# Cross attention: values held in TensorE on four column tiles, outputs turned back, and a new order of the work around them

## What is computed

```python
x = _layernorm(x + xattn(x, ctx, ctx, Wq, bq, Wk, bk, Wv, bv, Wo, bo))

def xattn(query, key, value, ...):          # 16 heads of 16 channels
    q, k, v = heads(query @ Wq + bq), heads(key @ Wk + bk), heads(value @ Wv + bv)
    scores = einsum('bhqd,bhkd->bhqk', q, k) / sqrt(16)
    x = einsum('bhqk,bhkd->bhqd', softmax(scores), v)
    return join_heads(x) @ Wo + bo
```

## Time and profile before

| | us |
|---|---|
| median of 3 runs | 1328.49 (1326.06 to 1329.64) |
| the profiled execution | 1323.78 |
| its span in the profile | 1321.5 |
| TensorE busy | 1012.9 (77%) |
| VectorE busy | 1027.7 (78%) |
| ScalarE busy | 742.6 (56%) |
| GpSimd busy | 610.1 (46%) |

### The profile page before, as it was taken

The page is one execution under the profiler, slowest core; times in us unless marked ns, Lnnn a source line. Parts: engine busy times, 40 slices in busy tenths (PEclk is TensorE's granted clock), DMA queues, the critical chain, the costliest instruction groups (busy, mean ns, idle before and its releaser), DMA issues.

```text
span 1321.5 us, 25653 instructions
## 1 busy us (share of the span) xinstructions
PE 1012.9 (77%) x7366; PEld 761.2 (58%) x7367; DVE 1027.7 (78%) x2235; ACT 742.6 (56%) x1866; POOL 610.1 (46%) x789
## 2 busy tenths in 40 slices
PE   0335786763698998986888889883799999999980
PEld 0233342432576776763566566652788888888870
DVE  6893899999888988965788888865477777777765
ACT  4784644430678888871455555540366666666650
POOL 3896787775244444431444455543232233322324
PEclk9755987886789989896999999996799999999995
DMA  5953100003133333312022222221011111111105
GB/s 185 383 195 156 48 0 32 0 32 104 55 123 131 117 108 108 108 43 75 1 85 84 83 83 83 79 76 40 25 38 38 36 40 40 34 36 40 40 27 190
DMA packets 51884, 105.69 MB, mean 80 GB/s; under 512 B 9809, under 2 KB 36433, under 8 KB 51329
## 3 DMA queue, kind: packets, MB, share of 16 engines
q1 hardware_dynamic: 47472, 92.39, 20.3%
q0 software_dynamic: 4368, 12.78, 3.2%
HBM read 73.06 MB, written 32.10 MB: 80 GB/s over the span
## 4 chain that ended last, share of the span: by engine, by line
PE 37%; DVE 26%; issue 14%; POOL 6%; ACT 6%; DMA 1%; DVEq 0%; POOLq 0%; SPq 0%; ACTq 0%
PE banks L1985 14%; PE banks L1995 10%; DVE mix_sums L671 4%; ACT att_probs L1484 3%; PE banks L1383 2%; POOL whole L1119 2%; DVE carry L661 2%; DVE whole_stat L227 2%; DVE carry L658 2%; PE banks L1352 2%; DVE kvq L1655 1%; ACT whole_level L1047 1%; PE banks L1360 1%; PE banks L1396 1%; DVE q_sin L1622 1%
## 5 line engine op out<-in xcount | busy, mean ns | idle before, releaser
L2068 DVE SCALAR_TENSOR_TENSOR expert_gate<-banks,expert_steps,expert_chunk 128x128 f32<-128x128 f32 x546 | 166.5, 347 | 96.8 <-ACT expert_chunk L2030 94.5
L1985 PE MATMUL banks<-expert_parts,levels 128*128 128x128 bf16 x3276 | 229.5, 221 | 8.0 <-issue 5.6
L1985 PEld LDWEIGHTS banks<-expert_parts,levels 128*128 x3276 | 203.4, 99 | 48.9 <-issue 21.2
L1995 PE MATMUL banks<-down,up 128*128 x546 | 176.2, 406 | 0.0
L2030 ACT COPY expert_chunk<-banks 128x256 f32<-128x256 f32 x273 | 101.7, 373 | 103.9 <-PE banks L1985 103.8
L2123 POOL DMA_INDIRECT chosen_d<-expert_y,expert_target x39 | 38.9, 998 | 203.9 <-ACT expert_y L2040 203.9
L519 PE MATMUL banks<-x_turned,w_rkv 128*128 128x512 f32 (+1 forms) x192 | 101.6, 690 | 38.9 <-DVE weight L652 38.4
L2034 ACT ACTIVATE silu<-expert_gate,expert_steps 128x128 f32<-128x128 f32 x273 | 110.6, 405 | 15.8 <-DVE expert_gate L2068 15.7
L414 PE MATMUL banks<-consts,level 128*128 128x128 f32 x154 | 35.6, 423 | 87.2 <-POOL level L397 87.2
L2075 DVE SCALAR_TENSOR_TENSOR up<-expert_gate,expert_steps,silu 128x128 f32<-128x128 f32 x273 | 94.6, 347 | 9.3 <-ACT silu L2034 9.3
L1119 POOL TENSOR_TENSOR whole<-whole_level,whole_stat 128x896 bf16<-128x896 f32 x32 | 53.2, 1684 | 102.1 <-DVE whole_level L1188 102.1
(11 more groups left out here) (237 smaller groups left out, 2541.6 us busy)
## 6 DMA issues: line engine op xcount, KB each, us to landing
whole_raw<-in_weight_jobs SPq DMA_DIRECT2D x16, 896.0 KB, 5.2
raw<-in_weight_jobs SPq DMA_DIRECT2D x11, 896.0 KB, 4.9
numbers_d<-turned SPq DMA_DIRECT2D x11, 896.0 KB, 5.1
levels_d<-whole_t SPq DMA_DIRECT2D x16, 448.0 KB, 2.7
levels<-levels_d SPq DMA_DIRECT2D x16, 448.0 KB, 3.6
down<-numbers_d SPq DMA_DIRECT2D x16, 448.0 KB, 4.4
finish_moe<-chosen_d SPq DMA_DIRECT2D x8, 512.0 KB, 7.3
normed_d<-normed_parts SPq DMA_DIRECT2D x16, 192.0 KB, 1.9
```

Source lines behind the costliest of these rows:

```text
L1985: last = pe.matmul(banks[:, at, (m * DC + c) * ROWS:(m * DC + c + 1) * ROWS], levels[:, bass.ds(expert * (2 * JOB) + (m * JOB + (f * DC + ...
L1995: last = pe.matmul(banks[:, Y + j, 0:D], up[j][:, f, :], down[:, bass.ds(expert * JOB + f * D, D)], start=(f == 0), stop=(f == FC - 1))
L2068: last = dve.scalar_tensor_tensor(out=gate[slot(j, f)][:, m, :], in0=halves(at)[:, m, 1, :], scalar=steps[j][:, m, 1, f:f + 1], in1=chunk[ ...
```

## The change

- **Sums.** `v_ones` is widened from 17 to 32 columns (the rest zero) and becomes the stationary operand; the 128 columns of the turned probabilities are moved. The four heads a = 0 to 3 write to the partition bands 32a of PSUM, so to four column tiles of the array. The results of a half (two sets of four heads) lie transposed in the free half of bank V.
- **Outputs turned back.** ScalarE copies them out (`take_outs`, one 128x256 copy a half, to `outs`), and TensorE turns them by two transposes a half (`turn_outs`), into bank HEADS, where `normalise` reads them with a stride of 32.
- **Order.** TensorE: `front` loses its part for the values (`front_v`) and moves ahead of `turn_heads` and behind `turn_probs(0)`; `join(n-1)` moves from the first part of the step to behind `turn_probs(1)` and `turn_outs(0)`, and waits for `take_outs(0, n)`. ScalarE: `take_outs(1, n-1)` leads the step, `back(n-1)` moves behind `take_qk`, `take_outs(0, n)` stands behind `round_part(1)`. GpSimd: `spread_keys` twice, then `add_bias`, then `scale`. VectorE: `normalise(n-1)` moves from the end of a step to behind `peaks(1)` of the next; the join's read (`read_joined`) moves behind the range reductions, and the layer norm (`norm_joined`) behind `peaks(0, n+1)`.

Left out of the diff: the constant `WIDE = 32`, two new semaphores and the last lines of VectorE's program, where `normalise`, `read_joined` and `norm_joined` are called for the last sequence.

```diff
@@ -763,11 +764,12 @@
         spread = [k.buffer(own, f"spread{h}", [QUAD, S]) for h in range(2)]
-        v_ones = [k.buffer(own, f"v_ones{j}", [XH, XK + 1]) for j in range(2)]
+        v_ones = [k.buffer(own, f"v_ones{j}", [XH, WIDE]) for j in range(2)]
         x_bias = [k.buffer(own, f"x_bias{j}", [D]) for j in range(2)]
...
         probs_t = [k.buffer(own, f"probs_t{h}", [HALF, S]) for h in range(2)]
+        outs = [k.buffer(own, f"outs{h}", [2, S]) for h in range(2)]
         total = k.buffer(own, "total", [XH])
@@ -887,8 +891,8 @@
             pe.wait_ge(rows_in[j], 32 * i + 32)
-            if not begin:
-                pe.wait_ge(heads_t_ready, n)
+            if not (isinstance(n, int) and n < 2):
+                pe.wait_ge(whole_read, ROUNDS * (n - 1))
             for c in range(DC):
@@ -904,9 +908,13 @@
             last.then_inc(qk_ready, 1)
-            if not begin:
+        def front_v(j, n):
+            if not (isinstance(n, int) and n == 0):
                 pe.wait_ge(v_read, n)
-                pe.wait_ge(joined_read, n)
+                pe.wait_ge(outs_ready, 2 * n - 1)
+            if not (isinstance(n, int) and n < 2):
+                pe.wait_ge(joined_read, n - 1)
             for c in range(DC):
@@ -930,33 +938,44 @@
-        def sums(j, h, n):
+        def sums(j, h, n, more):
             if h == 0:
-                pe.wait_ge(v_read, n + 1)
-                pe.wait_ge(heads_ready, n + 1)
+                pe.wait_ge(v_read, n + 1 + more)
+            else:
+                pe.wait_ge(joined_read, n + 1)
+            pe.wait_ge(outs_ready, 2 * n + h + 1)
             for m in range(2):
...
                     head = HALF * h + 4 * m + a
-                    last = pe.matmul(banks[:, HEADS, head * (XK + 1):(head + 1) * (XK + 1)], probs_t[h][:, 4 * m + a, :],
-                                     v_ones[j][:, head, :], start=True, stop=True)
+                    last = pe.matmul(banks[WIDE * a:WIDE * (a + 1), V, D + m * S:D + (m + 1) * S], v_ones[j][:, head, :],
+                                     probs_t[h][:, 4 * m + a, :], start=True, stop=True)
+            last.then_inc(outs_summed, 1)
+        def turn_outs(h, n):
+            if h == 0:
+                pe.wait_ge(heads_ready, n + 1)
+            pe.wait_ge(outs_ready, 2 * n + h + 2)
+            for m in range(2):
+                last = pe.transpose(banks[:, HEADS, (2 * h + m) * P:(2 * h + m + 1) * P], outs[h][:, m, :], k.ident)
             if h:
...
             pe.wait_ge(heads_ready, n + 2)
-            pe.wait_ge(x_t_ready, n + 1 + more)
+            pe.wait_ge(x_t_ready, n + 2 + more)
             pe.wait_ge(whole_read, ROUNDS * n + ROUNDS)
...
-        def join(j, n, more):
+        def join(j, n, taken):
             pe.wait_ge(heads_t_ready, n + 2)
-            pe.wait_ge(v_read, n + 1 + more)
+            pe.wait_ge(outs_ready, taken)
             for c in range(DC):
@@ -980,33 +999,41 @@
             if prev:
-                turn_heads(1 - j, n - 1, 1)
+                turn_outs(1, n - 1)
             turn_probs(0, n)
+            if more:
+                front(1 - j, n + 1, i + 1)
             if prev:
-                join(1 - j, n - 1, 1)
-            if more:
-                front(1 - j, n + 1, i + 1)
+                turn_heads(1 - j, n - 1, min(more, 1))
+            if more:
+                front_v(1 - j, n + 1)
             tiles(0)
-            sums(j, 0, n)
+            sums(j, 0, n, min(more, 1))
             tiles(1)
             turn_probs(1, n)
+            turn_outs(0, n)
+            if prev:
+                join(1 - j, n - 1, 2 * n + 2)
             if more:
...
             tiles(2)
-            sums(j, 1, n)
+            sums(j, 1, n, 0)
             tiles(3)
         front(0, 0, 0, True)
+        front_v(0, 0)
         scores(0, 0, 0, True)
         in_steps(step, pe)
-        turn_heads(1, B - 1, 0)
-        join(1, B - 1, 0)
+        turn_outs(1, B - 1)
+        turn_heads(1, B - 1, -1)
+        join(1, B - 1, 2 * B + 1)
...
         act.sem_inc(probs_t_ready, 2)
+        act.sem_inc(outs_ready, 1)
@@ -1032,6 +1059,10 @@
+        def take_outs(h, n):
+            act.wait_ge(outs_summed, 2 * n + h + 1)
+            act.copy(outs[h][:, :, :], banks[:, V, D:2 * D].rearrange("p (m s) -> p m s", m=2)).then_inc(outs_ready, 1)
         def back(j, n):
@@ -1062,7 +1093,7 @@
             if prev:
-                back(1 - j, n - 1)
+                take_outs(1, n - 1)
             collect(0, n)
@@ -1070,9 +1101,12 @@
                 take_qk(1 - j, n + 1)
+            if prev:
+                back(1 - j, n - 1)
             tiles(0)
...
                 round_part(1 - j, n + 1, 1)
+            take_outs(0, n)
             tiles(1)
@@ -1088,6 +1122,7 @@
         in_steps(step, act)
+        take_outs(1, B - 1)
         back(1, B - 1)
@@ -1122,12 +1157,12 @@
             make_whole(j, n)
+            if more:
+                spread_keys(1 - j, 0, n + 1)
+                spread_keys(1 - j, 1, n + 1)
+                add_bias(1 - j, n + 1, i + 1, not prev)
             if prev:
                 scale(1 - j, n - 1)
-            if more:
-                add_bias(1 - j, n + 1, i + 1, not prev)
-                spread_keys(1 - j, 0, n + 1)
-                spread_keys(1 - j, 1, n + 1)
@@ -1154,16 +1189,18 @@
             dve.wait_ge(heads_summed, n + 1)
-            all_heads = banks[:, HEADS, 0:XH * (XK + 1)].rearrange("p (h d) -> p h d", h=XH)
+            all_heads = banks[:, HEADS, :].rearrange("p (h d) -> p h d", h=XH)
             st.did(dve.reciprocal(total[:, :], all_heads[:, :, XK]))
...
-        def join(j, n, i):
+        def read_joined(j, n):
             dve.wait_ge(joined_ready, n + 1)
...
             dve.tensor_tensor(joined[j][:, :], banks[:, V, 0:D], x_bias[j][:, :], ALU.add).then_inc(joined_read, 1)
+        def norm_joined(j, n, i):
             dve.wait_ge(joined_read, n + 2)
@@ -1191,17 +1228,19 @@
             peaks(1, n)
+            if prev:
+                normalise(1 - j, n - 1)
             if more:
                 steps_of(1 - j, n + 1, i + 1 if prev else 0)
-            if prev:
-                join(1 - j, n - 1, i)
-            if more:
                 take_values(1 - j, n + 1)
...
                 range_of(j, n + 2, i + 2 - j)
+            if prev:
+                read_joined(1 - j, n - 1)
             if more:
                 peaks(0, n + 1)
-            normalise(j, n)
+            if prev:
+                norm_joined(1 - j, n - 1, i)
@@ -1209,6 +1248,7 @@
             dve.memset(v_ones[j][:, :, XK:XK + 1], 1.0)
+            dve.memset(v_ones[j][:, :, XK + 1:WIDE], 0.0)
         range_of(0, 0, 0)
```

More of the change, by code:

```diff
@@ L36 @@
 BAND = QUAD * XK
+WIDE = 32
 QH, KVH, HD = 8, 2, 128
@@ L802, in cross_stage @@
     probs_t_ready = k.semaphore("probs_t_ready")
+    outs_summed = k.semaphore("outs_summed")
+    outs_ready = k.semaphore("outs_ready")
     heads_summed = k.semaphore("heads_summed")
@@ L1218, in vector @@
         in_steps(step, dve, st, 2 * (5 + 6))
-        join(1, B - 1, TURNS - 1)
+        normalise(1, B - 1)
+        read_joined(1, B - 1)
+        norm_joined(1, B - 1, TURNS - 1)
         st.done(1, st.at)
```

## The result

The changed kernel takes 1367.64 us (median of 4 runs, 1366.91 to 1369.08); the kernel before, with a fourth run, 1329.01 us. The ratio is 1.0314, 95% interval 1.0273 to 1.0354: 3.1% slower. The sign and the place were as forecast; the size, 38.6 us, was 0.6 of the 64 us expected, and 1367.64 lies 0.4 us under the range's lower end.

A forecast was written before the change was run, and what follows sets the result against it. VectorE's in-order queue was taken as the bound. A first interval of 15.8 us plus 14 x 20.3 made 300.0 against 236.65 (+63.4); with ends +65 on 1323.8, 1388.7; the median 4.7 higher: 1393 us, range 1368 to 1425.

The forecast's parts named there:

- the range's lower end: Whole kernel: 1368 us, for a clock low in 10% and hand-overs some tenths shorter than taken.
- The bound before: Cross-attention stage: VectorE's in-order queue sets the pace, 15.78 us a step; freeing another engine wins under 1 us.
- The walk: One cross-attention step followed engine by engine with old durations: 15.74 us before, 19.47 after at the high clock.
- The loop: Cross-attention, clip to clip: ScalarE's late outputs copy holds TensorE's turn, join and next scores, VectorE waits; 19.47 us.
- rival 3: Cross-attention: VectorE stays the bound, step 15.74 us less 0.1, -2 to -3 us in all, 1326; chance 0.05.
- First term: Cross-attention step at the high clock: 15.74 us becomes 19.47.
- Second term: TensorE's clock in cross-attention: low 35% of a step at 2.4 us wholly low, adding 0.84 us: 20.3.
- the first interval: First of 15 intervals between clips, with no step before it, so neither join nor layer norm: 15.8 us.
- head and tail: Stage's ends: two memsets at the start +0.5 us, last copy, transposes and hand-overs +1 us.
- The sums: TensorE's sums on column tiles: a half falls from 1.91 us to 0.6.
- rival 4: TensorE's sums: column tiles don't run side by side, a half stays at 1.9 us; 1395 to 1405; chance 0.08.
- Spread keys ahead of the bias: GpSimd's new order in cross-attention: costs nothing, and the 0.76 us wait for the power stays.

The follow-up runs named there:

- b_pool_half: Kernel before with the second of GpSimd's two subtractions a step left out (the output is another one): 1309.0 us, ratio 0.9889.
- b_join_in_stall: Kernel before with only VectorE's order changed, layer norm cut in three, joined rows and first statistics ahead of the steps' subtraction: 1317.1 us, ratio 0.9947.
- a_outs_early: Changed kernel with the first half's copy of the outputs moved ahead of the six rounding activations on ScalarE: 1348.2 us, ratio 1.0178.
- a_scores_first: Changed kernel with the next scores ahead of turn and join on TensorE, VectorE reading joined rows behind that scores half: 1336.0 us, ratio 1.0074.
- a_both: Changed kernel with outputs copied ahead of the six activations and scores ahead of turn and join: 1337.4 us, ratio 1.0102.
- a_norm_late3: Changed kernel with the normalising of the heads moved behind the steps' small operations on VectorE: 1372.2 us, ratio 1.034.
- b_spread_first: Kernel before with only GpSimd's order changed to spread keys, bias, then the layer norm's power: 1371.4 us, ratio 1.0371.

## Why the prediction was right, and what was mis-sized

**The bound before.** VectorE in order, not TensorE: shown by b_pool_half and b_join_in_stall, each of which touched no TensorE instruction and made the kernel faster. One step of that part was wrong: "All that can be won by freeing another engine is 15 x 0.04, under 1 us." The walk took every busy microsecond of VectorE for its own work and counted one hole, of 0.76 us. With half of GpSimd's subtractions gone 16.7 us were won (1309.0 against 1325.7).

**The loop.** Each station of the walk is in the rows after, from the clip at 478.98, with the forecast in brackets: rounding of n+1 at 5.78 (6.40), `back` done at 7.94 (8.57), tile copy at 8.51 (9.10), outputs copied at 11.67 (12.27), joined rows at 13.12 (13.66), scores half at 14.19 (14.65), next clip at 18.72 (19.47). The order and what waits for what were right throughout, and a_outs_early and a_scores_first show that it is a cause and not a picture: 1348 and 1336 us where the same walk, set to the measured step, gave 1347 and 1337. It passed over one hole: it has the values at 7.2 us of the step (7.27 in the rows) but doesn't say that VectorE waits for them (1.53 us). A longer wait stood behind, so this cost the forecast little, but it spoilt rival 3's price: with the copy early a step was to take 15.74 us less 0.1. It took 17.1 in a_outs_early and 16.5 in a_both, and the values' wait of 1.5 us stands in those steps.

**First term mis-sized: the step at the high clock, 19.47 for 18.72.** "`normalise(n-1)` now comes before `steps_of`, 0.62 us" was wrong: it cost nothing. The subtraction behind it (line 238) had been taken for 1.13 us of work. It is 0.17 of work and a wait. In the kernel before it ends where GpSimd's second subtraction (line 1119) ends: 460.87 + 1.13 = 462.00 and, for the last of the pair, 458.65 + 3.33 = 461.98. Its row over the stage (shortest, median, longest ns) shows the scatter that work of fixed size can't have:

```profile
460.87 1.13 DVE L238 TENSOR_TENSOR whole_stat<-whole_stat 128x14 f32<-128x14 f32 x1
```

```profile
458.65 3.33 POOL L1119 TENSOR_TENSOR whole<-whole_level,whole_stat 128x896 bf16<-128x896 f32 x2 [6.64 <-DVE whole_level L1188]
...
465.02 0.72 POOL L1108 TENSOR_TENSOR x_bias<-x_in,bias_rows 128x256 f32<-128x256 f32 x1
```

```profile
L238 DVE TENSOR_TENSOR whole_stat<-whole_stat x16: 174/943/1140, 338.5 to 571.9; 128x14 f32<-128x14 f32 x16
```

After the change GpSimd's pair ends at 480.26 + 3.33 = 483.59, and the subtraction at 483.10 + 0.51 = 483.61:

```profile
480.26 3.33 POOL L1154 TENSOR_TENSOR whole<-whole_level,whole_stat 128x896 bf16<-128x896 f32 x2 [1.70 <-DVE whole_level L1225]
```

It is so throughout: in both kernels the last 14 of the 16 subtractions end 0.03 us behind a GpSimd subtraction. a_norm_late3 turned this round and b_pool_half took it away. The Trainium skill (SBUF — State Buffer, Who interferes with whom) has the rule: a VectorE instruction with two inputs in SBUF contends with a GpSimd instruction that reads SBUF, and one with at most one such input, outside the 2-port modes, doesn't. The trace agrees: `peaks`, which reads PSUM and at most one input in SBUF, takes 1.22 us beside the same GpSimd pair (479.99 and 481.34) and 1.22 us at 494.53, where GpSimd is idle.

The layer norm at the end of the step took 2.03 us (495.67 to 497.70), not 2.34. `crossed` is the difference, in its rows before and after (shortest, median, longest ns):

```profile
L1171 DVE TENSOR_SCALAR crossed<-joined,cross_ln x16: 412/760/811, 370.1 to 598.9; 128x256 f32<-128x256 f32 x16
```

```profile
L1208 DVE TENSOR_SCALAR crossed<-joined,cross_ln x16: 411/413/414, 384.7 to 646.7; 128x256 f32<-128x256 f32 x16
```

Before, it ran beside GpSimd's `x_bias` (465.02 above); after, GpSimd is idle there. In b_spread_first, which also leaves nothing on GpSimd beside it, its median is 413 ns; in b_pool_half, which keeps `x_bias` beside it, the mean is 720. That GpSimd's work beside it makes the difference those two runs show; that it is the same contention is argued. The two errors make 0.93 us, and hand-overs some tenths longer than I took gave 0.2 back.

**Second term mis-sized: the clock, 0.84 us a step for about 0.05.** I took 35% of the stage at the low clock, since waits would grow; the granted clock was 0.91, 18% low, less than the 22% before. In the step shown:

```profile
478.98:482.00 3.02, 2.77 (x17) 2.77 (x18) 2.89 (x4) 1.33 (x3) 1.74 (x2) 0.65 0.65 221
482.00:497.70 15.70, 9.66 (x87) 5.99 (x86) 10.66 (x19) 12.34 (x31) 4.90 (x5) 1.00 0.21 71
```

The low stretch ended at about 481, and TensorE then waits for `x_t` until 483.97 anyway: in this kernel a low clock in the first microseconds of a step was free. Two of fourteen steps took 19.24 and 19.27 instead of 18.7; in both the low stretch lay over `q`, `v` and the first tiles, 5.6 to 9.1 us behind the clip; the second:

```profile
522.00:525.50 3.50, 3.39 (x15) 2.53 (x13) 0.60 (x3) 2.24 (x8) 1.29 (x2) 0.51 0.23 69
```
So a low stretch cost 0.55 us at most, and seldom that. Two steps of the reasoning failed: to turn "more idle time" into "more low clock" (TensorE's idle time in the stage grew from 22.7 to 84.0 us, and the mean granted clock rose from 0.89 to 0.91), and low clock into a price without asking where in the step it lies. The Trainium skill (TensorE: Matmul & The Clock Gate, Loop structure matters more than you think), which the prediction cites, says that a long wait between matmuls costs the high clock. Here TensorE's waits between the clips grew, the longest from 1.7 to 2.3 us, and the share of low clock did not.

In sum: 14 x 0.75 = 10.5 and 14 x 0.79 = 11.1 too much, the first interval 0.8 too little (16.64 for 15.8), head and tail 2.5 too little (4.0 for 1.5). 65 - 10.5 - 11.1 + 0.8 + 2.5 = 46.7, the 46.5 of the stage. The rest of the way to 38.6 is the 2.5 us that the other stages gave back and the kernel before, whose median now lies 5.2 us above its profiled execution while the changed kernel's lies at its own (1367.64 and 1367.76). At the stage's start two operations of `steps_of` took 0.97 and 0.96 us beside GpSimd's spread keys, which is most of the head that I missed.

That 1367.64 lies so close to the range's lower end, 1368, is luck: the end stood for a clock low in 10% and hand-overs some tenths shorter than taken, and neither came true (18% low, hand-overs 0.2 us longer in all). The time got there by the subtraction's wait, the shorter layer norm, and low stretches that lay where they cost nothing.

**The other parts.** The sums: 0.64 us a half for the 0.6 taken, and their records start four at a time (four between 487.38 and 487.50, the next four between 487.50 and 487.61); four column tiles do run side by side, and rival 4 fell. The added transposes and copies cost what their neighbours had (0.41 and 0.36 us). Spread keys ahead of the bias: in the changed kernel neither TensorE's scores nor VectorE wait longer for GpSimd than before (0.76 us for the power), as said; in the kernel before it cost 3.7%.

## What to carry to other kernels

Walk one step of the new order with the durations of the old trace, station by station, before counting what an edit saves: here 2.5 us a step came off TensorE's sums, for which nobody waited, and one copy behind six activations gave away 1.5 us of every step. In an in-order queue ask of each added wait what stands behind it; moving the scores past it gave back three quarters of the loss. And where a small operation is long and its length varies, look for what ends at the same moment on another engine before taking its duration as work; that gap, filled, and a wait hidden in the same edit made the kernel before 0.5% faster.

## What was not expected of the hardware

A 128x14 subtraction on VectorE took from 0.17 to 1.14 us with the same operands' shape, ending 0.03 us behind GpSimd's subtraction in 14 of 16 steps, and the profile counts all of it as busy time. Sixteen fp32 matmul records (two for each of eight products) of 128 moving columns on four column tiles took 0.64 us with their 16 weight loads of 32 columns (0.38 us), against 1.04 us for eight transposes of the same width on the full array.
